# Eight-layer decoder block on one core: norms and score bounds moved in among the residual rows, fewer fillers, another ScalarE order

## The reference

```
x = x + tanh(g_xattn[0]) * linear_attention(layernorm(x), ctx)     # attn0
x = x + tanh(g_ffn[0])   * moe_top1_relu(layernorm(x))             # ffn0
x = x + tanh(g_xattn[1]) * attention_16_heads(layernorm(x), ctx)   # attn1
x = x + tanh(g_ffn[1])   * dense_8_experts_silu(layernorm(x))      # ffn1
x = x + tanh(g_xattn[2]) * one_head_attention(layernorm(x), ctx)   # attn2
x = x + tanh(g_ffn[2])   * moe_top1_gelu(layernorm(x))             # ffn2
x = x + tanh(g_xattn[3]) * attention_16_heads(layernorm(x), ctx)   # attn3
x = x + tanh(g_ffn[3])   * moe_top2_relu(layernorm(x))             # ffn3
```

## Time and profile before

| | us |
|---|---|
| median of 3 runs | 1987.97 (1986.66 to 1992.17) |
| the profiled execution's own time | 1972.97 |
| its span in the profile | 1971.2 |
| TensorE busy | 1848.1 (94%) |
| VectorE busy | 1402.6 (71%) |
| ScalarE busy | 1094.5 (56%) |
| GpSimd busy | 730.8 (37%) |

### The profile page before, as it was taken

The page is one execution under the profiler, slowest core; times in us unless marked ns, Lnnn a source line. Parts: engine busy times, 40 slices in busy tenths (PEclk is TensorE's granted clock), DMA queues, the critical chain, the costliest instruction groups (busy, mean ns, idle before and its releaser), DMA issues.

```text
span 1971.2 us, 34855 instructions
## 1 busy us (share of the span) xinstructions
PE 1848.1 (94%) x11498; PEld 1557.3 (79%) x11498; DVE 1402.6 (71%) x2375; ACT 1094.5 (56%) x2003; POOL 730.8 (37%) x754
## 2 busy tenths in 40 slices
PE   7889996999999999999999999999998997898993
PEld 5579995877888888888888888888767997686993
DVE  4767777678777777777777777777766664866664
ACT  5548883685545555555555555455424774573771
POOL 6023331556434344353443534434002232342231
PEclk9999998999999999999999999999989999899997
DMA  4246662001000000100000000031114551203544
GB/s 126 71 144 200 200 176 76 2 17 33 17 32 16 32 32 16 32 16 32 32 16 32 21 27 32 16 116 50 30 38 150 147 147 50 71 2 118 176 138 142
DMA packets 113578, 138.95 MB, mean 70 GB/s; under 512 B 15332, under 2 KB 101606, under 8 KB 113504
## 3 DMA queue, kind: packets, MB, share of 16 engines
q1 hardware_dynamic: 105952, 121.70, 20.2%
q0 software_dynamic: 7552, 16.24, 2.8%
HBM read 117.22 MB, written 24.90 MB: 72 GB/s over the span
## 4 chain that ended last, share of the span: by engine, by line
PE 80%; DVE 10%; ACT 4%; issue 3%; DMA 2%; ACTq 0%; DVEq 0%; SPq 0%; POOL 0%; POOLq 0%
PE ps L688 43%; PE ps L949 10%; PE ps L950 10%; PE ps L951 10%; PE ps L695 2%; PE ps L882 1%; ACT ps L1595 1%; DVE xs L1799 1%; ACT wsplit L1556 1%; DVE bn L1719 1%; DVE wsplit L2180 1%; DVE lnx L1702 1%; PE ps L1149 1%; PE ps L1108 1%; DVE h_lo L2161 1%
## 5 line engine op out<-in xcount | busy, mean ns | idle before, releaser
L688 PE MATMUL ps<-h_hi,wsplit 128*128 128x512 f32 (+3 forms) x2016 | 588.5, 350 | 1.8 <-DVE xT L1947 1.3
L688 PEld LDWEIGHTS ps<-h_hi,wsplit 128*128 128x128 f32 x2016 | 366.7, 188 | 48.7 <-DVE xT L1947 1.8
L688 PE MATMUL ps<-h_lo,wsplit 128*128 128x512 f32 (+3 forms) x1008 | 352.5, 350 | 0.0
L574 POOL TENSOR_TENSOR wsplit<-wraw,zero 128x256 fp32r<-128x256 f32 (+2 forms) x160 | 150.9, 960 | 497.0 <-PE ps L951 407.7
L1477 ACT ACTIVATE lnx<-ps 128x512 f32<-128x512 f32 x384 | 229.3, 598 | 106.3 <-PE ps L951 63.6
L688 PE MATMUL ps<-xTh,wsplit 128*128 128x256 f32 (+2 forms) x992 | 254.9, 311 | 8.0 <-DVE h_lo L2161 4.4
L1486 ACT ACTIVATE h_act<-h_act 128x512 f32<-128x512 f32 x192 | 120.9, 629 | 211.8 <-DVE h_act L1925 211.7
L1947 DVE TENSOR_TENSOR xT<-xT,ps 128x1024 f32<-128x1024 f32 x124 | 151.3, 1220 | 117.7 <-PE ps L688 117.7
L1490 ACT ACTIVATE h_hi<-ps 128x512 fp32r<-128x512 f32 x256 | 152.6, 596 | 142.1 <-PE ps L688 139.8
L2161 DVE TENSOR_TENSOR h_lo<-ps,h_hi 128x256 fp32r<-128x256 f32 (+2 forms) x248 | 117.7, 475 | 151.3 <-ACT h_hi L1599 150.1
L1934 DVE TENSOR_TENSOR ps<-h_act,ps 128x512 f32<-128x512 f32 x256 | 177.4, 693 | 44.3 <-PE ps L951 30.2
(11 more groups left out here) (289 smaller groups left out, 3580.3 us busy)
## 6 DMA issues: line engine op xcount, KB each, us to landing
wraw<-in_L_w SPq DMA_DIRECT2D x124, 512.0 KB, 3.9
wraw<-in_L_ffn_Wg SPq DMA_DIRECT2D x32, 256.0 KB, 2.7
wraw<-in_L_ffn_Wu SPq DMA_DIRECT2D x32, 256.0 KB, 3.0
wraw<-in_L_ffn_Wd SPq DMA_DIRECT2D x32, 256.0 KB, 3.6
x_tok<-lnx SPq DMA_DIRECT2D x12, 512.0 KB, 4.1
lnx<-y_tok SPq DMA_DIRECT2D x12, 512.0 KB, 5.9
y_tok<-lnx SPq DMA_DIRECT2D x3, 2048.0 KB, 13.8
wat<-in_attn SPq DMA_DIRECT2D x16, 256.0 KB, 4.8
```

The source lines that it names most:

```text
L574: return pool.tensor_tensor(out_, in_, zero[:, :].to_broadcast(shape), ALU.add)
L688: return pe.matmul(out_, lhsT, rhs, start=start, stop=stop)
```

## The change

It moves work of VectorE, ScalarE and TensorE at the four places, and it takes fillers out. At the first routing, 20 and 20 fillers become 6 and none, and ScalarE splits two pieces of weights before it normalises tiles 4 to 7 and copies groups 0 and 1 before it normalises tiles 8 to 11. In `mha`, VectorE does the mask's bounds and `bound`, `maxima` of tile 0 ahead of the last group's rows, and `bound` of tile 1 ahead of the norm of group 2; TensorE computes tile 1's scores ahead of the turn of group 2, and turns group 3 only after `step(0)`. In ffn1's last loop VectorE now normalises groups 0, 1 and 2 and computes the keys; attn2 turns each group just ahead of its query, into banks of its own, without the 24 fillers. In attn2's loop it normalises groups 0, 1 and 2 for ffn2, and the 40 fillers at the end become 10 with a wait for the last residual tile.

```diff
                 for g in range(NG):
-                    if g >= 2:
-                        fill(3, 20)
+                    if g == 2:
+                        fill(3, 6)
                     turn_group(1, g)
...
@@ ScalarE, attn0
                     group_rstd(NG + 2 * s, s)
+                    if s == NG - 2:
+                        for q in range(2):
+                            act.wait_ge(w_in[q], 16 * (LOADS["ffn0"][q] + 1))
+                            act.activation(whi[:, 0, q, :], wraw[:, q, :], ACT.Copy).then_inc(w_hi, 1)
+                    if s == NG - 1:
+                        copy_group(1, 0)
+                        copy_group(1, 1)
                     if s > 0:
                         norm_tiles(0, GROUP * (s - 1), GROUP * s)
-                copy_group(1, 0)
-                copy_group(1, 1)
...
@@ TensorE, mha
                 fill(7, 6)
-                turn_group(n, 2)
-                turn_group(n, 3)
                 query(1)
                 scores(1)
-                pe.wait_ge(xt_done, NG * (n + 1))
-                fill(7, 10)
+                turn_group(n, 2)
+                pe.wait_ge(xt_done, NG * n + NG - 1)
+                fill(7, 6)
                 step(0, 0, first=True)
+                turn_group(n, 3)
...
@@ TensorE, attn2
-                pe.wait_ge(x_done, NT * n - 2)
-                fill(0, 24)
...
                 turn(0)
+                query(0)
                 turn(1)
-                query(0)
                 query(1)
+                scores(0)
                 turn(2)
+                query(2)
                 turn(3)
-                scores(0)
-                query(2)
                 query(3)
...
-                fill(7, 40)
+                fill(7, 10)
+                pe.wait_ge(x_done, NT * (n + 1))
...
@@ VectorE, mha
-                for g in range(NG):
+                for g in range(NG - 1):
                     add_rows(layer - 1, n - 1, g, split=True)
                     if g > 0:
                         norm_group(n, g - 1)
+                bounds_of_mask()
+                bound(0, 0)
+                maxima(0, 0)
+                add_rows(layer - 1, n - 1, NG - 1, split=True)
+                bound(1, 1)
+                norm_group(n, NG - 2)
+                maxima(1, 1)
...
@@ VectorE, ffn1's last loop
+                    if i == 5:
+                        dve.wait_ge(zeroed, 1 + 16 * 3)
+                    if i == 12:
+                        keys_of_attn2()
+                    if i in (5, 10, 14):
+                        norm_group(n + 1, (5, 10, 14).index(i))
...
@@ VectorE, attn2's last loop
+                    if i in (7, 11, 15):
+                        norm_group(n + 1, i // 4 - 1)
```

More of the change, by code:

```diff
@@ L1432, in mha @@
                 query(0)
+                copy_group(n, 1)
+                query(1)
                 norm_rstd(n, 2)
-                copy_group(n, 1)
+                exps(0, 0)
+                copy_group(n, 2)
                 norm_rstd(n, 3)
-                copy_group(n, 2)
+                step(0, 0)
                 copy_group(n, 3)
-                query(1)
-                exps(0, 0)
-                step(0, 0)
                 with act.Fori(1, NT - 4, 2) as i:
@@ L1649, in attn2 @@
                 copy(0)
+                query(0)
                 copy(1)
-                query(0)
+                norm_rstd(n, NG - 1)
                 query(1)
                 copy(2)
-                copy(3)
                 query(2)
                 exps(0)
+                copy(3)
                 query(3)
@@ L1873, in mha @@
                         norm_group(n, g - 1)
+                bounds_of_mask()
[5 more added lines that the diff above has]
+                maxima(1, 1)
                 next_stats(n - 1, NT - 1)
                 norm_moments(n, NG - 1)
-                bounds_of_mask()
                 norm_group(n, NG - 1)
-                for j in range(2):
-                    bound(j, j)
-                    maxima(j, j)
                 step(0, 0, first=True)
@@ L1903, in mha, with keys_of_attn2 @@
                     norm_group(n + 1, NG - 1)
+            def keys_of_attn2():
+                dve.wait_ge(in_a2, 48)
+                dve.wait_ge(a2_pool, 3)
+                dve.wait_ge(a2_kv, 1)
+                dve.tensor_scalar(khT[:, :, :], ps[0:HD, 7, 0:P].rearrange("p (b s) -> p b s", b=B), bh[:, 1:2], 0.25, ALU.add, ALU.mult).then_inc(a2_kvb, 1)
+                for b in range(B):
+                    dve.tensor_tensor(vh[:, b, 0:HD], ps[:, 6, b * HD:(b + 1) * HD], bvh[:, :], ALU.add).then_inc(a2_kvb, 1)
             def ffn1(n):
@@ L2140, in moe @@
                 nth, cap, items, tiles = MOE.index(layer), CAP[layer], ITEMS[layer], IR[layer] // P
-                if layer:
+                if layer == 2:
+                    norm_group(n, NG - 1)
+                elif layer == 3:
                     norm(n)
@@ L2238, in heads @@
                                           ALU.mult).then_inc(a2_oh, 1)
-                dve.wait_ge(zeroed, 1 + 16 * 3)
-                norm_group(n, 0)
-                norm_group(n, 1)
-                dve.wait_ge(in_a2, 48)
-                dve.wait_ge(a2_pool, 3)
-                dve.wait_ge(a2_kv, 1)
-                dve.tensor_scalar(khT[:, :, :], ps[0:HD, 7, 0:P].rearrange("p (b s) -> p b s", b=B), bh[:, 1:2], 0.25, ALU.add, ALU.mult).then_inc(a2_kvb, 1)
-                for b in range(B):
-                    dve.tensor_tensor(vh[:, b, 0:HD], ps[:, 6, b * HD:(b + 1) * HD], bvh[:, :], ALU.add).then_inc(a2_kvb, 1)
-                norm_group(n, 2)
-                norm_group(n, 3)
+                norm_group(n, NG - 1)
                 dve.wait_ge(in_mask, 16 * MASKS[2])
```

28 lines of the change are left out of this document (16 added, 12 removed).

## The result

| | us |
|---|---|
| before, median of 5 runs | 1986.66 (1983.97 to 1992.17) |
| after, median of 5 runs | 2001.60 (2001.42 to 2004.87) |
| ratio, 95% interval | 1.0088 (1.0073 to 1.0104) |
| the profiled execution of after, span | 2001.42, 1999.4 |

The change makes the kernel slower, by 14.9 us between the medians (0.75%) and by 0.9% in the ratio on record, which isn't the quotient of the two medians. I had forecast 3 us. The time lies just beyond the upper end of my range and almost exactly on the slower rival's 2001.7. The same kernel before takes 1971 to 1973 us in some sets of runs and 1985 to 1987 us in others, each set on one chip, and by the length of ffn0's loop the profile shown before is of the first kind and that of after of the second.

What follows compares the result with a forecast made beforehand. TensorE, busy 94% of the span, was taken to bound the kernel, fillers included. Terms -3.5 + 0 + 2.0 + 4.7 + 0 gave +3.2 us on 1987.97: 1991.2, forecast as 1991, range 1980 to 2001.

Steps and rivals of the forecast that it cites:

- First routing, -3.5: First routing: `r_p` earlier, 5.1 us gained at full clock, 2.0 at clock 0.50; middle taken, 3.5 us gained.
- attn1 0, attn3 +2.0: Attention starts: group 2's later turn and shorter following work leave attn1 unchanged and make attn3 2.0 us slower.
- 0.3 us lost if it doesn't: Start of attn1: 353.3 + 2.9 = 356.2 against 355.90 if the clock doesn't stay up.
- attn2's start, +4.7: Start of attn2: exposed copies and low clock make it slower, 4.7 us as the middle of 2.3 and 7.
- Turn 0 and query 0 at half speed: Start of attn2: without the 24 fillers these two run slow, adding 0.95 + 1.8: 5 us late.
- with turn 1 and query 1 too, about 7: Start of attn2, upper end: the second turn and query also at half speed, about 7 us late.
- attn2's end, 0: End of attn2: 0.3 to 0.4 us gained at full clock, up to 5 us cost at low level; 0 taken.
- Turn 3 needs the last norm, at 1491.5 ... so it is hidden: End of attn2: the last turn comes at 1492.4, after the norm it needs, so that norm costs nothing.
- The bound of 5 us that I gave for the clock: End of attn2: at the low level four turns (+0.95 each) and the logits between cost up to 5 us.
- Carrying over the 15 us: Whole kernel: plain runs lie 15.0 us above the profiled execution's 1972.97; the same difference was assumed after the change.
- Half the clock everywhere: The slower rival: low clock at all the changed places, +13.7 us, 2001.7 us; chance 0.30.
- The early start pays: The faster rival: attn2's turns begin 3.3 us earlier and copies cost nothing; -6.4 us in all, 1981.6; chance 0.22.

Runs made afterwards that it cites:

- change_again: The whole change measured once more against before, on the chip where its parts were run: ratio 1.0070.
- only_attn2_end: Before with only attn2's end edited (ten fillers and a wait instead of forty, three norms in the residual loop), against before: ratio 1.0030, median +5.9 us.
- before_again: The kernel before, unchanged, measured once more against before: ratio 0.9997.
- attn2_start_old_order: Before with attn2's start as changed (no 24 fillers, early norms), but TensorE and ScalarE in the old order, against before: ratio 0.9990.

## Why the prediction was wrong

My sum of +3.2 us fell short of change_again's places by 10.9 us: 5.8 at attn2's end, 2.0 at attn1, 2.1 at attn3, 1.6 at attn2's start, and -0.6 at the routing.

**First routing, -3.5.** Right: -4.0 to -5.1 in six profiles, of which up to 1.6 us appear in unchanged code. With the shift of 2.2 us taken off, turn 3 stood at 87.5, where I had it at 87.4. The low clock came, but ended during this turn: from its start to `r_p` it was 4.3 us, not the 6.7 that I put for the low level, and so the gain lay near the full-clock end. No run separates the missing fillers from ScalarE's order.

**attn1 0, attn3 +2.0.** The mechanism was right, the idle time ahead of group 2's turn and 0.50 behind it. The sizes were too small, +1.0 to +2.0 and +3.5 to +4.1. With this run's shift of 4.4 us taken off, group 2's turn stood at 346.0 instead of my 344.0. Two of VectorE's terms were too short: the wait ahead of `bound`, 1.37 us instead of 0.3, and the last four residual tiles with their statistics, 4.3 us instead of 3.2. And the base was a draw, a matter of chance: "0.3 us lost if it doesn't" compared with a profile in which attn1 had the low level and attn3 had not. In kernels with unchanged attn1 and attn3 it is more often the other way round. The sum over both places hardly suffers from that, each term by itself does.

**attn2's start, +4.7.** Right in mechanism, +6.3 in the whole change and +8.2 alone. "Turn 0 and query 0 at half speed" was one occurrence; the level fell again before turn 2 and query 2. My end "with turn 1 and query 1 too, about 7" was added up wrongly, since another 0.95 + 1.8 on top of 5 gives 7.8, and the middle of 2.3 and 7.8 is 5.1. It named the wrong instructions as well. I also put the loss on the fillers and on the order; the runs showed it to be the order's alone.

**attn2's end, 0.** This is the step that failed: "Turn 3 needs the last norm, at 1491.5 ... so it is hidden", and "I take 0". It cost 5.8 us. I followed VectorE and TensorE and left out ScalarE, whose queue holds the copy of groups 0 and 1 behind a deviation and three pieces of weights. Before, the pieces ended when the turn of group 0 did, so nothing of it showed in a wait. Three norms, 4.1 us, now stand in front of the moments and made that chain late: in only_attn2_end the logits came 4.2 us later, and the low level behind the wait added 1.5. The bound of 5 us that I gave for the clock was nearly the right size for another cause: in only_attn2_end the turn of groups 0 and 1 was at full speed, and of four turns and the logits only one turn and the logits beside it ran at the low level.

**The sum.** With +2.0, +6.3, +5.8 and +4.1 against -4.1 it is +14.1, measured +14.9 in the medians and 1.0070, +13.7, on the second chip. Carrying over the 15 us between the profile and the plain runs was right, though I had no reason for it: before_again, profiled among the slower sets, takes 1986.26 us.

**The rivals.** "Half the clock everywhere" had the time to 0.1 us, and that is luck: its routing term was 2.1 us too high (-2.0 against -4.1) and its attn1 term 1.7 us too low, and at attn2's end it had another mechanism. "The early start pays" needed TensorE without exposed copies; attn2_start_old_order shows that this was to be had, with another order.

## What to carry to other kernels

When work is moved on one engine, follow every engine that hands over at that place, also the one that shows no wait. A queue whose pieces end just as they are needed has no slack, no time to spare, and the profile doesn't print slack. Where one engine hands its result to another and waits to get it back, put other work in between: turn, turn, query, query had no gap where turn, query, turn, query had one each time, and the lower clock behind the gaps doubled the price. Fillers over waits of 2.0 and 3.7 us brought nothing when they went, and fillers added in gaps of 1.4 to 2.3 us brought nothing either, but 24 fillers in the idle times of 3.5 and 4.5 us that the edits of `mha` had opened gave 3.4 us back in the medians. Look first at what ends the time after them.

## What the hardware showed that I had not expected

The same program is 13 us (0.7%) slower on some chips: medians of before were 1971.35 to 1972.84 us in three sets of rounds on three chips and 1985.10 and 1986.66 us in two. Whether it is the chip or the hour is not shown, since no chip has sets of both kinds. The time goes into the loops of ffn0, ffn2 and ffn3, 6.2 + 4.7 + 0.9 us in before_again, in ffn0 with the clock at 1.00. There ScalarE stands idle for up to 1.7 us ahead of a copy whose turn has ended, and the view names no instruction that released it (`<-remote`); what it waits for stays open.

Which of the two attention starts runs at half clock changes without a change of their code, at attn3 (2.2 us) between two executions of the same kernel, with idle times ahead of 1.4 to 2.3 us: a place whose clock was granted in one profile can't be counted on, in either direction.
